# A relative-position term on TensorE: two queries in 96 rows of the array, or eight queries in three times 128 rows

## What is computed

```
idx = r[None, :] - r[:, None] + (MAX_LEN - 1)      # r = arange(1024), MAX_LEN = 512
rel = rel_emb[idx]
qk = einsum('bhld,bhrd->bhlr', q, k) / sqrt(16)
qk = qk + einsum('bhld,lrd->bhlr', q, rel)
att = softmax(qk)
```

## Time and profile before

| | us |
|---|---|
| median of 3 runs (lowest and highest) | 6519.43 (6518.75 to 6520.47) |
| profiled execution | 6501.09 |
| its span | 6499.3 |
| busy: TensorE matmul, VectorE, GpSimd, ScalarE | 6203.9, 5036.1, 3640.9, 3134.0 |

### The profile page before, as it was taken

How to read it: one execution, slowest core, us unless ns; L and a number is a source line. 1 busy time by engine, 2 the same in 40 slices (tenths; PEclk the granted TensorE clock), 3 DMA queues, 4 the chain that set the end, 5 groups by cost and what they waited for, 6 DMA issues and landing times.

```text
span 6499.3 us, 408509 instructions
## 1 busy us (share of the span) xinstructions
PE 6203.9 (95%) x178176; PEld 5783.0 (89%) x178176; DVE 5036.1 (77%) x10289; ACT 3134.0 (48%) x5145; POOL 3640.9 (56%) x4707
## 2 busy tenths in 40 slices
PE   5999999999999999999999999999999999999997
PEld 4999899999999999999999999899999999998997
DVE  3777777777787777777777777777777777777776
ACT  2444444444444444444444444444444444444444
POOL 5555555555565555555555555555555555555555
PEclk8999999999999999999999999999999999999998
DMA  3111121111212112121111211112111121211210
GB/s 86 37 44 50 37 58 37 51 45 35 58 36 59 35 35 61 35 60 33 42 56 35 60 36 48 45 39 58 35 52 43 35 58 38 59 35 33 62 35 27
DMA packets 570089, 296.73 MB, mean 46 GB/s; under 512 B 384176, under 2 KB 534688, under 8 KB 568624
## 3 DMA queue, kind: packets, MB, share of 16 engines
q1 hardware_dynamic: 568624, 272.86, 15.2%
HBM read 184.46 MB, written 88.60 MB: 42 GB/s over the span
## 4 chain that ended last, share of the span: by engine, by line
PE 75%; DVE 15%; issue 6%; DVEq 3%; POOLq 1%; POOL 0%; SPq 0%; ACT 0%; DMA 0%
PE sc L665 19%; PE sc L681 13%; PE sc L660 11%; PE pw L691 11%; DVE r L960 6%; PE pm L672 6%; PE pm L712 4%; PE pw L698 4%; PE pw L712 4%; DVE nm L969 3%; DVE ceq L1008 2%; DVEq L971 2%; DVE y2n L926 1%; DVE dm L983 1%; PE pm L703 1%
## 5 line engine op out<-in xcount | busy, mean ns | idle before, releaser
L960 DVE TRANSPOSE_TENSOR_REDUCE r<-sc 128x32 f32<-128x1024 f32 x2048 | 2547.5, 1244 | 49.2 <-PE sc L665 48.3
L665 PE MATMUL sc<-rm,tw 96*128 96x32 f16 x65536 | 2288.9, 176 | 58.1 <-issue 58.1
L845 ACT ACTIVATE prob<-sc 128x1024 f32<-128x1024 f32 x2048 | 2095.7, 1023 | 237.9 <-PE sc L681 173.7
L665 PEld LDWEIGHTS sc<-rm,tw 96*128 96x128 f16 x65536 | 1976.9, 97 | 64.7 <-issue 64.3
L660 PE MATMUL sc<-qm,ks 96*128 96x64 f16 x32768 | 1635.2, 193 | 29.9 <-DMA ks<-qk_s 15.1
L969 DVE TENSOR_REDUCE nm<-pm 16x32 f16<-16x256 f32 x2048 | 840.5, 410 | 932.2 <-PE pm L672 931.4
L660 PEld LDWEIGHTS sc<-qm,ks 96*128 96x128 f16 x32768 | 1380.8, 98 | 105.7 <-issue 35.2
L681 PE MATMUL sc<-nmm,pick 128*128 128x64 f16 x32768 | 1305.7, 194 | 1.4 <-DVE nmm L972 1.4
L681 PEld LDWEIGHTS sc<-nmm,pick 128*128 128x128 f16 x32768 | 1150.9, 98 | 126.9 <-issue 103.2
L691 PE MATMUL pw<-prob,vs 128*32 128x128 f32 x32768 | 1110.2, 276 | 100.2 <-DVE nm L969 89.9
L691 PEld LDWEIGHTS pw<-prob,vs 128*32 128x32 f32 x32768 | 835.2, 110 | 158.5 <-DVE nm L969 119.8
(11 more groups left out here) (129 smaller groups left out, 5753.9 us busy)
## 6 DMA issues: line engine op xcount, KB each, us to landing
raw<-qk_s SPq DMA_DIRECT2D x774, 64.0 KB, 2.5
tw<-tw_s SPq DMA_DIRECT2D x512, 72.0 KB, 2.0
v_s<-vpad SPq DMA_DIRECT2D x136, 256.0 KB, 3.4
vs<-v_s SPq DMA_DIRECT2D x64, 512.0 KB, 3.7
ks<-qk_s SPq DMA_DIRECT2D x384, 64.0 KB, 2.4
xin<-x SPq DMA_DIRECT2D x138, 128.0 KB, 2.1
qk_s<-qkh SPq DMA_DIRECT2D x272, 64.0 KB, 1.7
qk_s<-qkl SPq DMA_DIRECT2D x272, 64.0 KB, 1.6
```

The source lines that it names most:

```text
L665: last = mm(out3[:, :, 2 * k:2 * k + 2], tw[:, jp, u:u + P], rm[:, i, k, :, :], start=False, stop=False, skip_group_check=True)
L845: A(prob[:, jp % 2, :, :, i * IW:(i + 1) * IW], sc[:, 2 * buf:2 * buf + 2, :].rearrange("p c (h i) -> p c h i", i=IW), ACT.Exp).then_inc(s ...
L960: v.tensor_reduce(r1[:, :], sc[:, 2 * buf:2 * buf + 2, :].rearrange("p c (h i) -> p (c h) i", i=IW), axis=AX.X, op=ALU.max, apply_transpos ...
```

## The change

The stationary operand of the relative term takes all 128 rows. Eight queries have 8 x 48 = 384 rows, that is three stationaries of 128. The boundaries fall inside of a query: the first stationary holds queries 0, 1 and two thirds of 2, the second the rest of 2, then 3, 4 and a third of 5, the third the rest of 5, then 6 and 7 (`RUNS`: first query and number of queries of each). Queries 2 and 5 are each added up from two matmuls. For 32 queries there are then 12 matmuls, eight of 48 columns and four of 64, where there were 16 of 32.

`rm` becomes 160 columns for eight queries instead of 128, written by three instructions over 128 rows in place of one over 96. `tw` and `raw` are kept in three layers of 128 rows (`RP`), so `load_raw` issues 24 DMAs a tile instead of six, the table's layout in DRAM 24 instead of six, and a window is one DMA of three times 128 rows instead of one of 96. `qm` is made as before, from the first layer of `raw`.

```diff
+OCT = 8
+RP = 3
+RUNS = ((0, 3), (2, 4), (5, 3))
+RCOL = (0, 3, 7)
+RN = 10
-            for s in range(2):
-                for k, part in enumerate(SPLIT_ST):
-                    r = (3 * s + k) * HD
-                    sp.dma_start(tw_s[r:r + HD, :], t_s[part, :, 1 - s:1 - s + NU]).then_inc(s_tws, 16)
-            sp.wait_ge(s_tws, 6 * 16)
+            for k in range(RP * OCT):
+                q, part = divmod(k, 3)
+                r = k % OCT * HD
+                sp.dma_start(tw_s[k // OCT, r:r + HD, :],
+                             t_s[SPLIT_ST[part], :, OCT - 1 - q:OCT - 1 - q + NU]).then_inc(s_tws, 16)
+            sp.wait_ge(s_tws, RP * OCT * 16)
...
-                sp.dma_start(tw[:, jp, :], tw_s[:, bass.ds(u, TWC)] if not isinstance(u, int)
-                             else tw_s[:, u:u + TWC]).then_inc(s_tw[jp], 16)
+                src = tw_s.rearrange("s p u -> p s u")
+                sp.dma_start(tw[:, :, jp, :], src[:, :, bass.ds(u, TWC)] if not isinstance(u, int)
+                             else src[:, :, u:u + TWC]).then_inc(s_tw[jp], 16)
...
-                for s in range(2):
-                    for k, part in enumerate(SPLIT):
-                        r = (3 * s + k) * HD
-                        src = qk_s[part, 0, b].rearrange("(h d) t -> d h t", d=HD)
-                        sp.dma_start(raw[r:r + HD, :, :], src[:, :, it * P:it * P + P] if isinstance(it, int)
-                                     else src[:, :, bass.ds(it * P, P)]).then_inc(s_raw, 16)
+                for k in range(RP * OCT):
+                    r = k % OCT * HD
+                    src = qk_s[SPLIT[k % 3], 0, b].rearrange("(h d) t -> d h t", d=HD)
+                    sp.dma_start(raw[r:r + HD, k // OCT, :, :], src[:, :, it * P:it * P + P]
+                                 if isinstance(it, int) else src[:, :, bass.ds(it * P, P)]).then_inc(s_raw, 16)
...
-                src = raw[:, :, i * IW:(i + 1) * IW]
-                g.tensor_tensor(qm[:, i, :, :], src, mask_q[:, :, :], ALU.mult)
-                g.tensor_tensor(rm[:, i, :, :, :].rearrange("p i h s -> p h i s"),
-                                src.rearrange("p h (i s) -> p h i s", s=2),
-                                mask_r[:, :, :].rearrange("p h (i s) -> p h i s", s=2),
-                                ALU.mult).then_inc(s_mask, 1)
+                g.tensor_tensor(qm[:, i, :, :], raw[0:ROWS, 0, :, i * IW:(i + 1) * IW], mask_q[:, :, :], ALU.mult)
+                for s, ((q, n), c) in enumerate(zip(RUNS, RCOL)):
+                    src = raw[:, s, :, i * IW:(i + 1) * IW].rearrange("p h (m e) -> p m h e", e=OCT)
+                    last = g.tensor_tensor(rm[:, i, :, c * H:(c + n) * H].rearrange("p m (h e) -> p m h e", e=n),
+                                           src[:, :, :, q:q + n],
+                                           mask_r[:, c:c + n].rearrange("p (a b e) -> p a b e", a=1, b=1)
+                                           .to_broadcast((P, IW // OCT, H, n)), ALU.mult)
+                last.then_inc(s_mask, 1)
...
-                for k in range(IW // 2):
-                    u = P - 1 - (i * IW + 2 * k) + c * P
-                    last = mm(out3[:, :, 2 * k:2 * k + 2], tw[:, jp, u:u + P], rm[:, i, k, :, :],
-                              start=False, stop=False, skip_group_check=True)
+                for m in range(IW // OCT):
+                    u = P - 1 - (i * IW + OCT * m) + c * P
+                    for s, ((q, n), r) in enumerate(zip(RUNS, RCOL)):
+                        last = mm(out3[:, :, OCT * m + q:OCT * m + q + n], tw[:, s, jp, u:u + P],
+                                  rm[:, i, m, r * H:(r + n) * H].rearrange("p (h e) -> p h e", e=n),
+                                  start=False, stop=False, skip_group_check=True)
```

More of the change, by code:

```diff
@@ L48, in sandwich_kernel @@
     v_s = nc.dram_tensor("v_s", ((B + 1) * TPB, P, H * 32), f32, kind="Internal").ap()
[L49 to L50 removed]
+    t_s = nc.dram_tensor("t_s", (2, HD, NU + OCT - 1), f16, kind="Internal").ap()
+    tw_s = nc.dram_tensor("tw_s", (RP, P, NU), f16, kind="Internal").ap()
     ctx = ExitStack()
@@ L65, in sandwich_kernel @@
         mask_q = sb("mask_q", [ROWS, H, IW], f16)
-        mask_r = sb("mask_r", [ROWS, H, IW], f16)
+        mask_r = sb("mask_r", [P, RN], f16)
         tri = sb("tri", [P, E, E])
@@ L91, in sandwich_kernel @@
         relf = sb("relf", [HD, NREL])
-        tf = sb("tf", [HD, NU + 1])
-        th = sb("th", [HD, NU + 1], f16)
-        tl = sb("tl", [HD, NU + 1], f16)
-        tw = sb("tw", [ROWS, NJP, TWC], f16)
+        tf = sb("tf", [HD, NU + OCT - 1])
+        th = sb("th", [HD, NU + OCT - 1], f16)
+        tl = sb("tl", [HD, NU + OCT - 1], f16)
+        tw = sb("tw", [P, RP, NJP, TWC], f16)
         ks = sb("ks", [ROWS, H // 2, L], f16)
         vs = sb("vs", [P, JC, H, 32])
-        raw = sb("raw", [ROWS, H, P], f16)
+        raw = sb("raw", [P, RP, H, P], f16)
         qm = sb("qm", [ROWS, NI, H, IW], f16)
-        rm = sb("rm", [ROWS, NI, IW // 2, H, 2], f16)
+        rm = sb("rm", [P, NI, IW // OCT, RN * H], f16)
         prob = sb("prob", [P, 2, 2, H, P])
@@ L496, in _ @@
             g.memset(mask_q[:, :, :], 1.0)
-            g.memset(mask_r[:, :, :], 1.0)
+            g.memset(mask_r[:, :], 1.0)
             g.memset(tri[:, :, :], 1.0)
@@ L520, in _ @@
             q4 = mask_q[:, :, :].rearrange("p (h s) i -> p h s i", s=2)
-            r4 = mask_r[:, :, :].rearrange("p h (i s) -> p h i s", s=2)
             keep(q4[:, :, 0, :], ALU.is_ge, half - 1, [[0, H // 2], [0, IW]], -1)
             keep(q4[:, :, 1, :], ALU.is_ge, -half, [[0, H // 2], [0, IW]], 1)
-            keep(r4[:, :, :, 0], ALU.is_ge, half - 1, [[0, H], [0, IW // 2]], -1)
-            keep(r4[:, :, :, 1], ALU.is_ge, -half, [[0, H], [0, IW // 2]], 1)
+            for (q, n), c in zip(RUNS, RCOL):
+                lo = q * half - c // 3 * P
+                keep(mask_r[:, c:c + n], ALU.is_ge, -lo, [[-half, n]], 1)
+                pool.drain()
+                keep(mask_r[:, c:c + n], ALU.is_ge, lo + half - 1, [[half, n]], -1)
             keep(tri[:, :, :], ALU.is_gt, 0, [[1, E], [-1, E]], 0)
@@ L943, in _ @@
             normal(xn[:, :], xin[:, :], mv0, rs0).then_inc(s_xn, 1)
-            v.memset(tf[:, 0:1], 0.0)
-            v.tensor_copy(tf[:, 1:1 + MAX_LEN], relf[:, NREL - MAX_LEN:NREL])
-            v.tensor_copy(tf[:, 1 + MAX_LEN:1 + MAX_LEN + NREL], relf[:, :])
-            v.tensor_copy(tf[:, 1 + MAX_LEN + NREL:NU + 1],
+            v.memset(tf[:, 0:OCT - 1], 0.0)
+            v.tensor_copy(tf[:, OCT - 1:OCT - 1 + MAX_LEN], relf[:, NREL - MAX_LEN:NREL])
+            v.tensor_copy(tf[:, OCT - 1 + MAX_LEN:OCT - 1 + MAX_LEN + NREL], relf[:, :])
+            v.tensor_copy(tf[:, OCT - 1 + MAX_LEN + NREL:NU + OCT - 1],
                           relf[:, NREL - 1:NREL].to_broadcast((HD, NU - MAX_LEN - NREL)))
```

6 lines of the change are left out of this document (2 added, 4 removed).

## The result

The changed kernel takes 6628.64 us in the median (6623.63 to 6637.52, four runs), the kernel before 6519.56 (6518.75 to 6520.47) beside it: a ratio of 1.0169, 95% interval 1.0151 to 1.0186. It is 109 us slower. The forecast was 31 us slower: the direction and the range held, but the loss was three and a half times the one forecast, 78 us more.

A forecast was written before the change was run, and what follows sets the result against it. TensorE, VectorE and a loop over GpSimd with 0.86 us of room bound the kernel. Tiles at +0.08 us give +10, start-up +21: +31 on 6501 is 6532, plus 18 to the runs' median: 6550 us; range 6415 to 6700.

The forecast's parts named there:

- gain of the matmuls: From `xn` to `yn` in an ordinary tile: eleven chunks that count, each 0.087 us shorter, save 0.96 us.
- VectorE held up by GpSimd: Behind `xn` in an ordinary tile: VectorE's two-input instructions wait for GpSimd's later run; 0.4 us taken, between nothing and 0.54.
- GpSimd's loop: Ordinary tile, through `x1`, masks, `rs0`, `xn`: masks add 2.28 us against 0.86 of room; tile 49.68 us, +0.90.
- The price's form: GpSimd's three `rm` pieces: 1.97 ns a column plus 175 ns fixed, 553 + 679 + 553 = 1785 ns; +0.57 us a mask.
- Rival A: GpSimd keeps up: a mask costs only +0.28 us, with no fixed part; 6415 us; chance 0.2.
- The matmuls: TensorE's relative matmuls: 48 columns at the 25.6 ns pace of 32; a chunk falls from 410 to 323 ns, saving 87.
- rival C: TensorE's matmuls don't get cheaper: all at 29.6 ns, 6602 us; no gain at all adds 156 + 21 us; chance 0.13.
- The third tile: Every third tile, bound by TensorE's own way: saves 1.65 us to 49.58; GpSimd sets about the same, 49.68; -1.55.
- Loads in the tiles: SyncE's 18 more DMAs a tile, 8.6 us longer, under a cover of 22 us: put at nothing.
- rival D: In the tiles, loads come late, the 22 us cover gone; every microsecond over is 126 us; chance 0.05.
- Start-up: Before the first scores: 18 more layout DMAs cost 11.3 us and 18 `raw` loads 9.5; together +21 us.

The follow-up runs named there:

- e9: The changed kernel with `qm` written by ScalarE, two activations a strip, in place of one GpSimd instruction: 6426.83 us, ratio 0.9879.
- e3: The kernel before with one more GpSimd instruction of 192 columns in each mask, into a spare tile: 6641.56 us, ratio 1.0186.
- e5: The changed kernel without the third `rm` piece of each mask, so part of the sum is left out: 6414.61 us, ratio 0.9858.
- e15: The changed kernel with `qm` by ScalarE and relative matmuls writing their columns in one run (no valid scores): 6386.00 us, ratio 0.9803.
- e11: The changed kernel, relative matmuls writing 48 or 64 columns in one run instead of 16 short ones (no valid scores): 6631.51 us, ratio 1.0192.
- e4: The kernel before with the changed kernel's query loads, table layout and window loads alone: 6584.81 us, ratio 1.0098.
- e13: The changed kernel, windows of table layers two and three loaded only before the first tile (scores partly changed): 6606.76 us, ratio 1.0143.

## Where the forecast was right, and the step that failed

The forecast's own sum for an ordinary tile, beside what the trace has (medians):

| | forecast | measured |
|---|---|---|
| `yn` to `x1` | 1.12 | 1.09 |
| `x1` to `rs0`, with the masks | 15.29 + 2.28 = 17.57 | 17.51 |
| `rs0` to `xn` | 0.04 | 0.04 |
| `xn` to `yn`: gain of the matmuls | 31.51 - 0.96 | 31.14 in e9 (-0.37) |
| and VectorE held up by GpSimd | +0.4 | 31.45, so +0.31 |
| sum | 49.68 | 50.1 (mean 50.19) |

**GpSimd's loop: right.** It does what the forecast said it would, with `xn` as the place, and at the price: +0.59 a mask against +0.57, and the way from `x1` to `rs0` longer by 17.51 - 15.27 = 2.24 against 2.28. e3, e5 and e9 show the cause from three sides: the masks' work put into the kernel before costs 1.9%, a part of it taken out of the changed one gives 3.1%, and moved to ScalarE 2.9%.

**The price's form: wrong, its sum right.** 553 + 679 + 553 = 1785 ns was taken, 513 + 607 + 691 = 1811 measured. The first two pieces are cheaper than forecast and the last, as large as the first, is dearer by 138 ns, so that the sum fits is partly luck. Why the last is dearer wasn't tested. In size it is the first; it starts at an odd query (5) and comes last. Rival A, the price by columns alone (+0.28), is out.

**The matmuls: the step that failed.** "For 48 columns I take the pace of 32 as they are nearest to it": 25.6 ns, and the saving of 87 ns a chunk. Measured 29.9 and 47 ns, rival C's pace. The term 11 x 0.087 = 0.96 behind `xn` is 0.37 instead. 11 x 0.040 = 0.44 of the difference is the pace; the remaining 0.15 is the count: 0.37 is eight chunks' worth, and with 81 ns saved in e15 it is 31.51 - 30.81 = 0.70, nearly nine. The cause is the output in short runs. e11 takes them away and nothing else, and its ordinary tiles without a clock drop take 49.77 us where the forecast had 49.68 and the changed kernel takes 50.12. Its time did not follow, by the clock drops in 32 tiles, which the forecast had no term for either. With the matmuls sized rightly the forecast would have been rival C's 6602.

**The third tile: failed with it.** It was put at 49.68, as GpSimd's loop sets it too. It takes 50.5 in the median and 50.75 in the mean. With 19 x 0.047 = 0.89 in place of 1.65, TensorE's own way is 51.23 - 0.89 = 50.3, just above the loop's 50.1. VectorE comes to `xn` 0.56 behind `rs0` in the mean (0.06 in ordinary tiles), so both bound it by turns, and in 7 of 41 the clock drops, to 51.97. What the rest of it is stays open; it isn't the pauses at the loop's end, which are 52.0 us in all and were 58.1.

**Loads in the tiles, put at nothing: wrong.** As was said, they aren't late: in the traces of e4 and of the changed kernel no engine's wait in the tiles ends with a DMA, so rival D is out. But their traffic costs some 40 us in e4. In the changed kernel some 17 may be the windows' (e13, overlapping intervals). **Start-up: right**, 20.9 us against 21, with 11.5 more of waiting for `xin` and 9.4 more for `raw`'s DMAs.

By the means, the miss is (2 x 0.51 + 1.07) / 3 = 0.70 us a tile, 88 us in 126 tiles. The profiled execution's span grew by 122.6 against a forecast of 31, so 92 were missed in it: the tiles account for them.
